# Delta-rule attention on one core: TensorE's projection work goes ahead of the second scores in slot 6, and ahead of the turned probabilities in slot 8

## The chip, the core and the metric

The program runs on one core of a Trainium2 chip. The metric is the device time of one execution in microseconds (us). The names of the engines in the profile: PE is TensorE (PEld its weight loads), DVE is VectorE, ACT is ScalarE, POOL is GpSimd, SP is SyncE.

## What is computed

Four layers with a residual each, on 1024 tokens of width 256: attention with a memory, a mixture of 16 experts, retention, and a mixture of 8 experts. Only the first is touched. Cut to what matters, with 16 heads of width 128 and segments of 64 tokens:

```python
def step(carry, seg):                       # 8 segments one after the other, 2 batches
    mem, z = carry
    qq, kk, vv = seg
    sigma_q = jax.nn.elu(qq) + 1.0
    scores = jnp.einsum('bhsk,bhtk->bhst', qq, kk) / scale
    scores = jnp.where(causal_mask, scores, -jnp.inf)
    att_dot = jax.nn.softmax(scores, axis=-1) @ vv
    att_mem = sigma_q @ mem / (sigma_q @ z)
    sigma_k = jax.nn.elu(kk) + 1.0
    delta = vv - sigma_k @ mem / (sigma_k @ z)
    mem_new = mem + jnp.einsum('bhsk,bhsv->bhkv', sigma_k, delta)
    z_new = z + sigma_k.sum(axis=-2, keepdims=True).transpose(0, 1, 3, 2)
    att = beta * att_mem + (1.0 - beta) * att_dot
    out = att.reshape(Bsz, SEG, H * DV) @ Wo
```

In front of it stand the projections of the normalised input to q, k and v.

## The kernel before

The attention goes through 8 stages, called 0 to 7 here: four turns, each with four heads, and two halves in each turn, one for each batch of 512 tokens. In the code `n = 2 * it + half` is the stage. The turns 1 and 2 are a loop in the program, turns 0 and 3 are written out.

A stage has 16 slots, `m` = 0 to 15, two for each of the 8 segments. The four heads are two groups `g` of two. Ahead of each slot TensorE reads the memory of one group (`read_memory`, L587) and adds the last segment's update to the memory of the other (`update_memory`, L597). This is the recurrence: ScalarE copies the memory out of its bank (L784), TensorE reads it, VectorE takes the reciprocal of the denominator (L911) and forms the difference from v (L917), TensorE updates.

A slot adds other work, which belongs to three stages at once:

- The stage itself: scores of two heads (`scores`, L608) in slots 0 and 6, into bank L[0]; VectorE masks them and takes the row's maximum in slots 1 and 7 (`mask_scores`, L927 and L932); GpSimd subtracts it (L469); ScalarE takes the exponential in slots 4 and 9 (L799); VectorE sums it in slots 5 and 10 (L936); GpSimd multiplies by the inverse (L478). TensorE turns these probabilities in slots 8 and 12 (`turn_probs`, L614), into L[0] and L[1], and ScalarE copies them in slots 9 and 13 (L804). TensorE multiplies them by v in slots 10 and 14 (L622).
- The stage behind: its readings are turned in slots 1 to 4 (L628), VectorE adds them one slot later (`add_reading`, L946), and its output projection is in slots 12 to 15 (L636).
- The stage ahead: `AHEAD_AT` gives projection unit u to slot u, for u = 0 to 11. A unit is six 128x512 matmuls (L233 to L235). Units 0 to 3 are the q of the four heads, 4 to 7 the k, 8 to 11 the four tiles of v. Slots 7 to 10 also turn the key feature of head 0 to 3 (`turn_sigma_k`, L574). Slot 7 is project 7, turn 0, and slot 8 is turn 1, project 8. Two banks serve all of this: units 0, 2, 4, 6 and 8 and turn 0 go to A[0], units 1, 3, 5 and 7 and turn 1 to A[1].

ScalarE empties the banks in the slot after (`copy_ahead`): of each q or k unit an exponential (L769) and a copy (L770), of a turned feature a copy (L778). VectorE forms the feature two slots after the unit (`sigma`, L889, then L902 for q, or L895 and L900 for k). The exponential of unit u goes to a buffer that unit u - 2 used, so ScalarE waits for the feature of unit u - 2.

Each engine takes its instructions in the order of the code. What TensorE waits for ahead of the steps that the change touches is:

```python
pe.wait_ge(qk_copied, 8 * n + u - 1)        # project, unit u = 2 to 7: the copy of unit u - 2
pe.wait_ge(skt_copied, 4 * n + 1)           # project, unit 8: the copy of turn 0
pe.wait_ge(qk_copied, 8 * n + h + 7)        # turn_sigma_k, h = 0, 1: the copy of unit 6, 7
pe.wait_ge(sigma_ready, 8 * n + h + 5)      # turn_sigma_k: VectorE's feature of that head
```

The second scores wait for `att_ready` (the fourth `add_reading`, VectorE's slot 5), and the turned probabilities for `masked` (L927 of VectorE's slot 7) and `p_ready`. Stage 0 has no stage behind, stage 7 none ahead.

Of the kernel before, what the change touches and what calls it, by code (L numbers as in the profile page):

```python
# [229 lines left out]
def split3(pe, out, stationary, moving, first, last, **kw):  # L230

    (sh, sl), (mh, ml) = stationary, moving
    pe.matmul(out, sh, mh, start=first, stop=False, **kw)  # L233
    pe.matmul(out, sh, ml, start=False, stop=False, **kw)  # L234
    return pe.matmul(out, sl, mh, start=False, stop=last, **kw)  # L235


def delta_attention(nc, outer, norm, carried, x, ident, ident_ready, scratch, x_in, Wq, Wk, Wv, Wo, betas, mask_in,
# [12 lines left out]
    with ExitStack() as ctx:  # L251
# [3 lines left out]
        def sem(name):  # L255
            signals.append(nc.alloc_semaphore(name=name))
            return signals[-1]

        def bank(name):
# [61 lines left out]
        sc_ready, masked, max_ready, shifted, exp_ready = (  # L321
            sem("scores_ready"), sem("scores_masked"), sem("max_ready"), sem("scores_shifted"), sem("exp_ready"))
        sum_ready, inv_ready, p_ready = sem("exp_sum_ready"), sem("exp_sum_inverted"), sem("probs_ready")
        pT_ready, pTs_ready, bt_ready, bt_copied = (
            sem("probsT_ready"), sem("probsT_copied"), sem("local_ready"), sem("local_copied"))
        at_ready, att_ready, wo_ready, y_copied = (
            sem("readingT_ready"), sem("attT_ready"), sem("out_ready"), sem("out_copied"))
# [38 lines left out]
        with nc.Block() as block:  # L366
# [154 lines left out]
            def _(pe):  # L521
# [13 lines left out]
                def project(n, half, u, free=None, at_start=None):  # L535

                    b = A[PROJECT_BANK[u]] if at_start is None else at_start
                    if free is not None:
                        pe.wait_ge(*free)
                    if u % 4 == 0:  # L540
                        pe.wait_ge(low_done, 3 * n + u // 4 + 1)
                    if at_start is not None:
                        pass
                    elif 2 <= u < 8:
                        pe.wait_ge(qk_copied, 8 * n + u - 1)
                    elif u == 8:
                        pe.wait_ge(skt_copied, 4 * n + 1)
                    elif u > 8:
                        pe.wait_ge(v_copied, 4 * n + u - 8)
                    for k in range(KD):  # L550
                        if u < 8:
                            i, h = u // 4, u % 4
                            cols = slice(half * HALF, (half + 1) * HALF)
                            last = split3(pe, b[:, :],
                                          (w_high[i][:, k, h * DK:(h + 1) * DK], w_low[i][:, k, h * DK:(h + 1) * DK]),
                                          (xh[:, k, cols], xl[:, k, cols]), k == 0, k == KD - 1)
                        else:
                            j = half * TPH + u - 8
                            last = split3(pe, b[:, :], (xh[:, k, j * P:(j + 1) * P], xl[:, k, j * P:(j + 1) * P]),
                                          (w_high[0][:, k, :], w_low[0][:, k, :]), k == 0, k == KD - 1)  # L560
                    last.then_inc(proj_ready, 1)
# [39 lines left out]
                def scores(n, half, pp):  # L601

                    for s in range(STEPS):
                        for hh in range(GROUP):
                            h, pair, par = GROUP * pp + hh, s // 2, s % 2
                            seg = slice((half * STEPS + s) * SEG, (half * STEPS + s + 1) * SEG)
                            at = (hh * TPH + pair) * SEG
                            last = pe.matmul(L[0][par * SEG:(par + 1) * SEG, at:at + SEG], qT[:, h, seg], kT[:, h, seg],  # L608
                                             start=True, stop=True)
                    last.then_inc(sc_ready, 1)  # L610

                def turn_probs(n, pp, hh):
                    for t in range(TPH):
                        last = pe.transpose(L[hh][:, t * P:(t + 1) * P], probs[:, hh * TPH + t, :], ident[:, :])  # L614
                    last.then_inc(pT_ready, 1)

                def local(n, half, pp, hh):

                    h = GROUP * pp + hh
                    pe.wait_ge(pTs_ready, 4 * n + h + 1)  # L620
                    for t in range(TPH):
                        last = pe.matmul(L[hh][:, t * P:(t + 1) * P], v[:, half * TPH + t, h * DK:(h + 1) * DK],  # L622
                                         pTs[hh][:, t * P:(t + 1) * P], start=True, stop=True)
                    last.then_inc(bt_ready, 1)

                def turn_reading(half, h):
                    for t in range(TPH):
                        last = pe.transpose(L[READINGS_BANK[h]][:, t * P:(t + 1) * P], read[:, half, h, t, :], ident[:, :])  # L628
                    last.then_inc(at_ready, 1)
# [10 lines left out]
                def slot(it, half, m, first, last):  # L640

                    n = 2 * it + half
                    ahead, behind = not (last and half), not (first and not half)
                    if m == 0:
                        if behind:
                            pe.wait_ge(bt_copied, 4 * n - 1)
                        scores(n, half, 0)
                    if m == 6:
                        if behind:
                            pe.wait_ge(att_ready, 4 * n)  # L650
                        pe.wait_ge(masked, 2 * n + 1)
                        scores(n, half, 1)
                    if behind and m in READINGS_AT:
                        h = READINGS_AT[m]
                        if h == 0:
                            pe.wait_ge(bt_copied, 4 * n)
                            for g in range(2):
                                pe.wait_ge(read_ready[g], STEPS * n)
                        elif h == 1:
                            pe.wait_ge(masked, 2 * n + 1)  # L660
                        else:
                            pe.wait_ge(att_ready, 4 * n - 4 + h - 1)
                        turn_reading(1 - half, h)
                    if m == 8:
                        pe.wait_ge(p_ready, 4 * n + 2)
                        pe.wait_ge(masked, 2 * n + 2)
                        turn_probs(n, 0, 0)
                        turn_probs(n, 0, 1)
                    if m == 12:
                        pe.wait_ge(p_ready, 4 * n + 4)  # L670
                        for hh in range(2):
                            pe.wait_ge(bt_copied, 4 * n + hh + 1)
                            turn_probs(n, 1, hh)
                    if m in (10, 14):
                        for hh in range(2):
                            local(n, half, (m - 10) // 4, hh)
                    if ahead:
                        for what, u in AHEAD_AT.get(m, ()):
                            if what == "turn":
                                turn_sigma_k(n + 1, 1 - half, u)  # L680
                                continue
                            free = None
                            if u == 0:
                                free = v_copied, 4 * n + 4
                            elif u == 1:

                                free = (skt_copied, 4 * n + 4) if first else (y_copied, n - 1)
                            project(n + 1, 1 - half, u, free)
                    out_at = OUT_AT if ahead else LAST_OUT_AT
                    if behind and m in out_at:  # L690
                        if m == min(out_at):
                            pe.wait_ge(att_ready, 4 * n)
                            if ahead:
                                pe.wait_ge(skt_copied, 4 * n + 8)
                            else:
                                pe.wait_ge(y_copied, n - 1)
                        project_out(1 - half, out_at[m])
# [36 lines left out]
                n = STAGES  # L734
# [1405 lines left out]
```

## Time and profile before

| | |
|---|---|
| time, median of 3 runs | 724.89 us (722.25 to 725.99) |
| span of the profiled execution, first to last instruction | 721.6 us |
| TensorE busy, matmuls | 659.8 us, 91% |
| VectorE busy | 405.8 us, 56% |
| ScalarE busy | 340.2 us, 47% |
| GpSimd busy | 309.3 us, 43% |
| a stage of the attention, stages 1 to 6 | 52.1 to 52.2 us |

Of the profiled execution the page gives the span alone, so this stands for its own time; it lies 3.3 us under the median and 0.65 us under the fastest of the three runs. The stage's length is the distance of the same instruction in neighbouring stages (L608 of slot 6 starts at 158.82, 211.01 and 263.12 us). Shares of the whole span are means over layers with different limits; the attention ends by about 450 us, and the change lies between 57 and 380 us.

### The profile page before, as it was taken

What the parts mean: (1) busy time and instruction counts of PE and PEld (TensorE: products, weight loads), DVE (VectorE), ACT (ScalarE), POOL (GpSimd) and SP (SyncE); (2) the same over time, 40 slices, a digit from 0 to 9 for tenths busy, and PEclk for the clock granted to TensorE, in tenths of its full rate; (3) what the DMA queues carried; (4) which work ended last, traced back from release to release, by engine and by line L of the source; (5) the groups of instructions that cost most, each with busy time, mean ns of one, the idle gap of its engine ahead of it and who ended that gap; (6) DMA issues with size and microseconds to landing.
All of it is one profiled execution on the core that took longest, in us unless ns stands there. A gap on an engine that the chain in (4) does not pass through costs nothing. (4 is left out here: it accounts for less than half of the span.)

```text
span 721.6 us, 12441 instructions
## 1 busy us (share of the span) xinstructions
PE 659.8 (91%) x4222; PEld 553.4 (77%) x4222; DVE 405.8 (56%) x1063; ACT 340.2 (47%) x836; POOL 309.3 (43%) x377
## 2 busy tenths in 40 slices
PE   3888999999999999999999997889999968996997
PEld 3767888988988979979979896776666556986754
DVE  6758487196295295494493646783222269555343
ACT  2655766567467567566566561323343321200221
POOL 4565462552453444353351111616666315200563
PEclk9999999999999999999999999799999979995999
DMA  8011010110210200200100131993233162009440
GB/s 263 30 41 49 30 32 30 55 36 7 64 32 2 65 29 0 65 29 12 55 1 1 42 78 65 334 368 95 92 94 90 52 216 80 1 29 365 135 121 23
DMA packets 29778, 57.90 MB, mean 80 GB/s; under 512 B 4670, under 2 KB 15904, under 8 KB 29728
## 3 DMA queue, kind: packets, MB, share of 16 engines
q1 hardware_dynamic: 22720, 42.03, 17.1%
q0 software_dynamic: 4896, 13.12, 6.2%
q10 hardware_dynamic: 2112, 2.10, 0.8%
q8 instruction: 30, 0.49, 0.3%
q14 instruction: 20, 0.16, 0.1%
HBM read 48.06 MB, written 10.09 MB: 81 GB/s over the span
## 5 line engine op out<-in xcount | busy, mean ns | idle before, releaser
L911 DVE RECIPROCAL denominators<-readings 128x2 f32<-128x2 f32 x128 | 21.2, 166 | 147.6 <-PE readings L587 146.9
L447 POOL TENSOR_TENSOR w_high<-xn,ones 128x256 fp32r<-128x256 f32 x84 | 53.9, 672 | 76.7 <-PE ahead L235 35.5
L587 PEld LDWEIGHTS readings<-memory_copy,sigma 128*128 128x128 f32 x512 | 75.2, 191 | 11.2 <-ACT memory_copy L784 2.2
L793 ACT ACTIVATE memory_reading<-readings,denominators 64x128 f32<-64x128 f32 x256 | 78.7, 357 | 6.0 <-DVE denominators L911 4.0
L587 PE MATMUL readings<-memory_copy,sigma 128*128 128x129 f32 x512 | 78.8, 276 | 2.2 <-ACT memory_copy L784 2.1
L784 ACT ACTIVATE memory_copy<-memory 128x258 f32<-128x258 f32 x128 | 50.2, 392 | 61.9 <-PE memory L597 47.9
L917 DVE SCALAR_TENSOR_TENSOR minus_delta<-readings,denominators,v 64x128 f32<-64x128 f32 x240 | 73.8, 347 | 4.5 <-DVE denominators L911 0.3
L597 PE MATMUL memory<-minus_delta,sigma_k_tokens 128*128 128x129 f32 x480 | 73.2, 275 | 0.0
L1221 POOL DMA_INDIRECT xs_e<-rows_e,gather_at_e x46 | 44.6, 969 | 54.3 <-DVE gather_at_e L1635 19.0
L1368 PE MATMUL up_e<-weights_e,xT_e 128*128 x184 | 66.4, 483 | 1.2 <-ACT xT_e L1497 1.2
L451 POOL TENSOR_TENSOR w_low<-xn,w_high 128x256 fp32r<-128x256 f32 x84 | 65.7, 813 | 1.6
L769 ACT ACTIVATE x<-ahead 128x512 f32<-128x512 f32 x60 | 35.9, 598 | 63.4 <-PE ahead L235 30.8
L636 PE MATMUL ahead<-wo,attT 128*128 128x256 f32 x256 | 64.4, 396 | 1.0 <-DVE attT L946 1.0
L597 PEld LDWEIGHTS memory<-minus_delta,sigma_k_tokens 128*128 128x128 f32 x480 | 63.0, 191 | 0.0
L1732 DVE TENSOR_TENSOR h_e<-gated_e,up_e 128x176 f32<-128x176 f32 x46 | 15.5, 338 | 80.7 <-ACT gated_e L1504 80.7
L478 POOL TENSOR_TENSOR xn<-scores,exp_sum_inverse 64x512 f32<-64x512 f32 x32 | 34.1, 1065 | 60.9 <-DVE exp_sum_inverse L938 59.1
L636 PEld LDWEIGHTS ahead<-wo,attT 128*128 128x128 f32 x256 | 58.9, 306 | 1.3 <-DVE attT L946 1.2
L1386 PE MATMUL down_e<-weights_e,hT_e 128*128 (+1 forms) x184 | 56.3, 405 | 0.0
L233 PE MATMUL ahead<-xh,w_high 128*128 128x512 f32 x120 | 53.0, 442 | 2.9 <-POOL w_low L451 1.9
L469 POOL TENSOR_TENSOR scores<-scores,score_max 128x512 f32<-128x512 f32 x16 | 16.8, 1048 | 82.4 <-DVE score_max L932 76.6
L1368 PEld LDWEIGHTS up_e<-weights_e,xT_e 128*128 128x128 f32 x184 | 31.2, 189 | 24.9 <-issue 15.0
L235 PE MATMUL ahead<-xh,w_low 128*128 128x512 f32 x120 | 48.0, 400 | 0.0
(282 smaller groups left out, 1444.6 us busy)
## 6 DMA issues: line engine op xcount, KB each, us to landing
weights_e<-experts SPq DMA_DIRECT2D x24, 608.0 KB, 12.1
xn<-L_attn_Wq SPq DMA_DIRECT2D x8, 512.0 KB, 3.9
xn<-L_attn_Wk SPq DMA_DIRECT2D x7, 512.0 KB, 3.8
xn<-L_attn_Wv SPq DMA_DIRECT2D x7, 512.0 KB, 3.8
wo<-L_attn_Wo SPq DMA_DIRECT2D x1, 2048.0 KB, 13.2
rows_e<-xn ACTq DMA_DIRECT2D x4, 512.0 KB, 10.4
x<-L_attn_x SPq DMA_DIRECT2D x4, 256.0 KB, 3.4
x<-L_attn_x SPq DMA_DIRECT2D x2, 512.0 KB, 3.5
```

The source lines that it names most:

```text
L233: pe.matmul(out, sh, mh, start=first, stop=False, **kw)
L235: return pe.matmul(out, sl, mh, start=False, stop=last, **kw)
L447: last = pool.tensor_tensor(w_high[i][:, :, of], w_stage[:, :, of], one, ALU.mult)
L451: last = pool.tensor_tensor(w_low[i][:, :, of], w_stage[:, :, of], fr(w_high[i][:, :, of]), ALU.subtract)
L587: last = pe.matmul(KQ[g][:, hh * MC:(hh + 1) * MC], sqk[:, GROUP * g + hh, pair, 2 * par:2 * par + 2, :], mz[g][:, hh, :], start=True, sto ...
L597: last = pe.matmul(MM[g][:, hh * MC:(hh + 1) * MC], skt[:, GROUP * g + hh, pair, :], dl[g][par][:, hh, :], start=False, stop=True, skip_gr ...
L636: last = pe.matmul(A[1][:, 0:D], rows[:, i::H], wo[:, i, :], start=(i == 0), stop=(i == H - 1))
L784: act.activation(mz[g][:, :, :], MM[g][:, 0:GROUP * MC].rearrange("p (h c) -> p h c", h=GROUP), ACT.Copy).then_inc(mem_copied[g], 1)
L793: last = act.activation(read[rows, half, GROUP * g + hh, pair, :], KQ[g][rows, hh * MC:hh * MC + DK], ACT.Copy, scale=nr[g][rows, hh:hh + 1])
L917: last = dve.scalar_tensor_tensor(out=dl[g][par][rows, hh, 0:DK], in0=KQ[g][rows, hh * MC:hh * MC + DK], scalar=nr[g][rows, hh:hh + 1], in ...
L1368: last = pe.matmul(GU[b % 2][:, 0:2 * INTER], xT[b % 2][:, k, :], flat[:, bass.ds(first + k * 2 * INTER, 2 * INTER)], start=k == 0, stop=k ...
L1386: last = pe.matmul(Y[b % 2][:, 0:D], hT[b % 2][0:count, k, :], flat[0:count, bass.ds(first + 4 * INTER + k * D, D)], start=k == 0, stop=k ...
```

## The change

In a slot with both, TensorE's second scores (slot 6) and first turns of probabilities (slot 8) now come behind the work for the stage ahead. Waits and instructions are the same, and no other engine's order differs.

```diff
--- before.py
+++ after.py
@@ -645,11 +645,6 @@
                         if behind:
                             pe.wait_ge(bt_copied, 4 * n - 1)
                         scores(n, half, 0)
-                    if m == 6:
-                        if behind:
-                            pe.wait_ge(att_ready, 4 * n)
-                        pe.wait_ge(masked, 2 * n + 1)
-                        scores(n, half, 1)
                     if behind and m in READINGS_AT:
                         h = READINGS_AT[m]
                         if h == 0:
@@ -661,11 +656,6 @@
                         else:
                             pe.wait_ge(att_ready, 4 * n - 4 + h - 1)
                         turn_reading(1 - half, h)
-                    if m == 8:
-                        pe.wait_ge(p_ready, 4 * n + 2)
-                        pe.wait_ge(masked, 2 * n + 2)
-                        turn_probs(n, 0, 0)
-                        turn_probs(n, 0, 1)
                     if m == 12:
                         pe.wait_ge(p_ready, 4 * n + 4)
                         for hh in range(2):
@@ -686,6 +676,16 @@
 
                                 free = (skt_copied, 4 * n + 4) if first else (y_copied, n - 1)
                             project(n + 1, 1 - half, u, free)
+                    if m == 6:
+                        if behind:
+                            pe.wait_ge(att_ready, 4 * n)
+                        pe.wait_ge(masked, 2 * n + 1)
+                        scores(n, half, 1)
+                    if m == 8:
+                        pe.wait_ge(p_ready, 4 * n + 2)
+                        pe.wait_ge(masked, 2 * n + 2)
+                        turn_probs(n, 0, 0)
+                        turn_probs(n, 0, 1)
                     out_at = OUT_AT if ahead else LAST_OUT_AT
                     if behind and m in out_at:
                         if m == min(out_at):
```

TensorE in slot 6 of a stage in the loop, before (readings and memory are the recurrence; ahead is the projection's bank, local the scores' bank; in brackets the semaphores that an instruction waits for):

```order
L597 MATMUL memory1<-minus_delta10,sigma_k_tokens 128x129 [waits delta_ready1]
L597 MATMUL memory1<-minus_delta10,sigma_k_tokens 128x129
L608 MATMUL local0<-kT,carried 64x64 [waits scores_masked,attT_ready]
L608 MATMUL local0<-kT,carried 64x64 x15
L545 REGISTER_ALU
L233 MATMUL ahead0<-xh,w_high1 128x512 [waits qk_copied]
```

The same place, of the change:

```order
L545 REGISTER_ALU
L233 MATMUL ahead0<-xh,w_high1 128x512 [waits qk_copied]
L234 MATMUL ahead0<-xl,w_high1 128x512
L235 MATMUL ahead0<-xh,w_low1 128x512
L233 MATMUL ahead0<-xh,w_high1 128x512
L234 MATMUL ahead0<-xl,w_high1 128x512
L235 MATMUL ahead0<-xh,w_low1 128x512
L608 MATMUL local0<-kT,carried 64x64 [waits scores_masked,attT_ready]
L608 MATMUL local0<-kT,carried 64x64 x15
L587 MATMUL readings1<-memory_copy1,sigma 128x129 [waits memory_copied1]
```

The 32 small matmuls of the scores, with their wait, now stand behind the six matmuls of unit 6 and directly ahead of slot 7's reading.

TensorE in slot 8 of that stage, before (xn holds the probabilities, sigma_k1 the key feature of head 1):

```order
L665 REGISTER_ALU
L666 REGISTER_ALU [waits probs_ready]
L614 MATMUL local0<-ident,xn 128x128 [waits scores_masked]
L614 MATMUL local0<-ident,xn 128x128 x3
L614 MATMUL local1<-ident,xn 128x128 x4
L569 REGISTER_ALU
L574 MATMUL ahead1<-ident,sigma_k1 128x128 [waits sigma_ready,qk_copied]
L574 MATMUL ahead1<-ident,sigma_k1 128x128 x3
L541 REGISTER_ALU
L547 ISA [waits w_split_done]
L233 MATMUL ahead0<-w_high0,xh 128x512 [waits sigma_k_copied]
```

The same place, of the change, from the last matmul of unit 8 on:

```order
L235 MATMUL ahead0<-w_high0,xl 128x512
L685 REGISTER_ALU
L686 REGISTER_ALU [waits probs_ready]
L614 MATMUL local0<-ident,xn 128x128 [waits scores_masked]
L614 MATMUL local0<-ident,xn 128x128 x3
L614 MATMUL local1<-ident,xn 128x128 x4
L587 MATMUL readings1<-memory_copy1,sigma 128x129 [waits memory_copied1]
```

Turn 1, with its wait for `qk_copied` (the copy of unit 7), and unit 8, with its wait for `sigma_k_copied` (the copy of turn 0), now stand directly behind slot 8's update, and the eight turns of the probabilities behind them.

## Rows read from the trace of the kernel before

**Rows 1.** The page's first lines: span, and TensorE's busy time

```profile
span 721.6 us, 12441 instructions
...
PE 659.8 (91%) x4222; PEld 553.4 (77%) x4222; DVE 405.8 (56%) x1063; ACT 340.2 (47%) x836; POOL 309.3 (43%) x377
```

**Rows 2.** Busy time by stretch: PE, PEld, DVE, ACT, POOL; then clock, DMA, GB/s

```profile
199.35:217.79 18.44, 17.50 (x136) 15.16 (x134) 17.66 (x42) 11.82 (x31) 9.49 (x11) 1.00 0.09 29
221.32:245.46 24.14, 24.14 (x159) 22.89 (x157) 7.34 (x26) 14.78 (x36) 12.22 (x18) 1.00 0.08 23
```

**Rows 3.** Timeline, TensorE, stage 3, slots 5 to 9: start, duration

```profile
209.80 0.61 PE L597 MATMUL memory<-minus_delta,sigma_k_tokens 128*128 128x129 f32 x4
211.01 1.20 PE L608 MATMUL local<-kT,carried 128*64 128x64 f32 x32 [0.60 <-DVE attT L946]
...
216.42 0.66 PE L574 MATMUL ahead<-ident,sigma_k 128*128 128x128 f32 x4 [0.34 <-ACT kT L770]
216.91 0.61 PE L587 MATMUL readings<-memory_copy,sigma 128*128 128x129 f32 x4
217.36 0.61 PE L597 MATMUL memory<-minus_delta,sigma_k_tokens 128*128 128x129 f32 x4
218.54 1.09 PE L614 MATMUL local<-ident,xn 128*128 128x128 f32 x8 [0.57 <-DVE scores L927]
...
221.32 0.61 PE L587 MATMUL readings<-memory_copy,sigma 128*128 128x129 f32 x4
```

**Rows 4.** Timeline, VectorE, stage 3, slots 6 and 7

```profile
214.82 0.43 DVE L900 COPY sigma<-sigma_k 128x512 f32<-128x512 f32 x1
...
217.34 0.43 DVE L900 COPY sigma<-sigma_k 128x512 f32<-128x512 f32 x1
217.79 0.69 DVE L927 SCALAR_TENSOR_TENSOR scores<-local,mask 128x512 f32<-128x512 f32 x1
```

**Rows 5.** Timeline, ScalarE, stage 3, slots 5 to 8

```profile
207.84 0.59 ACT L770 ACTIVATE kT<-ahead 128x512 f32<-128x512 f32 x1
...
215.28 0.60 ACT L769 ACTIVATE x<-ahead 128x512 f32<-128x512 f32 x1 [2.77 <-DVE sigma L900]
215.78 0.59 ACT L770 ACTIVATE kT<-ahead 128x512 f32<-128x512 f32 x1
...
217.80 0.60 ACT L769 ACTIVATE x<-ahead 128x512 f32<-128x512 f32 x1 [0.67 <-DVE sigma L900]
218.29 0.59 ACT L770 ACTIVATE kT<-ahead 128x512 f32<-128x512 f32 x1
218.77 0.60 ACT L778 ACTIVATE sigma_k_tokens<-ahead 128x512 f32<-128x512 f32 x1
```

**Rows 6.** Timeline, TensorE: slot 8's turns of the probabilities, stages 1 and 6

```profile
114.28 1.07 PE L614 MATMUL local<-ident,xn 128*128 128x128 f32 x8 [0.60 <-DVE scores L927]
...
374.92 1.06 PE L614 MATMUL local<-ident,xn 128*128 128x128 f32 x8 [0.60 <-DVE scores L927]
```

**Rows 7.** Timeline, stage 0, slots 7 to 9: TensorE, VectorE, ScalarE

```profile
65.94 1.63 PE L614 MATMUL local<-ident,xn 128*128 128x128 f32 x8 [2.58 <-DVE scores L927]
...
70.31 0.61 PE L587 MATMUL readings<-memory_copy,sigma 128*128 128x129 f32 x4
...
63.02 1.15 DVE L900 COPY sigma<-sigma_k 128x512 f32<-128x512 f32 x1
...
64.76 0.59 ACT L770 ACTIVATE kT<-ahead 128x512 f32<-128x512 f32 x1
65.24 0.60 ACT L778 ACTIVATE sigma_k_tokens<-ahead 128x512 f32<-128x512 f32 x1
```

**Rows 8.** Busy time by stretch, as rows 2: stage 0 and stage 3

```profile
64.00:66.00 2.00, 0.06 (x1) 0.09 (x2) 1.03 (x3) 1.73 (x4) 1.07 (x1) 1.00 0.71 241
66.00:68.00 2.00, 2.00 (x11) 2.00 (x12) 1.95 (x7) 0.74 (x3) 1.04 (x1) 0.57 0.00 0
...
216.00:218.00 2.00, 1.63 (x13) 1.36 (x12) 1.87 (x5) 1.33 (x5) 0.00 (x0) 1.00 0.00 0
```

## The prediction

> **What bounds the kernel now.** First the page: the span is 721.6 us and TensorE is busy 91% of it [rows 1]. TensorE looks like the bound, but that is a mean over four layers, and the change touches seven stages of one. So I read the timeline of one of them. Stage 3 stands for stages 1 to 6: slot 8's turned probabilities begin at 114.28 in stage 1 and at 374.92 in stage 6 [rows 6], which is 260.64 over five stages, 52.1 each.
>
> Busy time by stretch splits such a stage in two [rows 2]. From slot 9 to the next stage's slot 2 (221.32 to 245.46) TensorE is busy 24.14 of 24.14 us and VectorE 7.34: TensorE is the bound. From slot 2's end to slot 7 (199.35 to 217.79) VectorE is busy 17.66 of 18.44 and TensorE 17.50, with gaps: VectorE has become the bound. In this second part a wait of TensorE says only that TensorE is early for something of VectorE's; to start it on other work first ends nothing sooner unless VectorE, too, gets on.
>
> The timelines of the three engines show what TensorE meets there:
>
> - Slot 6: the update starts at 209.80 and the scores at 211.01, after 0.60 idle, for VectorE's L946 [rows 3]. A group of four such matmuls (two instructions) with work behind it takes 0.45 from start to start (216.91 to 217.36 [rows 3]), so without the wait they would have begun at 210.25: 0.76 is lost.
> - Slot 7: turn 0 waits 0.34 and starts at 216.42 [rows 3]. It needs the copy of unit 6, L770 from 215.78 for 0.59, until 216.37 [rows 5]. That stands behind unit 6's exponential, which started at 215.28 after 2.77 idle, for VectorE's L900 [rows 5] from 214.82 for 0.43, until 215.25 [rows 4].
> - Slot 8: the update starts at 217.36, the turned probabilities at 218.54 instead of 217.81 [rows 3]: 0.73 is lost. They waited for VectorE's mask, L927 from 217.79 for 0.69, until 218.48 [rows 4]. Slot 9 starts at 221.32 [rows 3].
>
> **The change, part by part.** No instruction is added or removed; six matmuls and 32 small ones change places in slot 6, eight turns change places with four turns and six matmuls in slot 8. No DMA and no other engine's queue is in it.
>
> *Slot 6.* Unit 6 needs the copy of unit 4, which was through at 207.84 + 0.59 = 208.43 [rows 5]; it starts at 210.25 with no wait. By the time that it is through, L946 has ended (it let the scores go at 211.01 [rows 3]), and the scores follow with none either. TensorE reaches the end of the slot 0.76 earlier. The scores themselves come a few tenths later, but VectorE takes them up only at 217.79 [rows 4], so that costs nothing; if VectorE were not so late, it would cost those tenths. Where do the 0.76 us go? To turn 0. Its chain (L900 until 215.25, exponential and copy on ScalarE until 216.37 [rows 4, 5]) has TensorE's unit 6 far behind it and is set by VectorE alone. VectorE was busy nearly without a break from slot 3 on [rows 2], and had no wait for TensorE to lose. So turn 0 stays at 216.42, and its wait grows from 0.34 to 1.10. Slot 6 is worth 0.00; at most 0.34 or 0.76 if VectorE's work itself shrank, for which I see no reason.
>
> *Slot 8.* The update still starts at 217.36, and from 217.81 TensorE is free. First in its queue is now turn 1. It needs the copy of unit 7: L770 from 218.29 for 0.59, until 218.88 [rows 5]. That again is VectorE's time: the exponential before it started at 217.80 after 0.67 idle, for L900, which ended at 217.34 + 0.43 = 217.77 [rows 4, 5]. With the 0.05 that lay between copy and turn in slot 7 (216.37 to 216.42), turn 1 starts at 218.93. Before, the first work started at 218.54, so the wait is 0.39 longer: the mask came out at 218.48, 0.40 before the copy. Queued behind turn 1 are unit 8, the turned probabilities, which could have run, and the recurrence's reading of slot 9, for which VectorE waits.
>
> Unit 8 needs the copy of turn 0: L778 from 218.77 for 0.60, until 219.37 [rows 5], so 219.42 at TensorE. Turn 1 takes 0.49 after a wait (turn 0: 216.42 to 216.91 [rows 3]), which is 218.93 to 219.42. This wait is just covered; without the turn ahead of it, it would cost another 0.49.
>
> The three pieces took 218.54 to 221.32 = 2.78 in the old order, the probabilities after a wait [rows 3]. In the new order it is turn 1 that follows a wait. I have no row for these pieces in the new order, so I bound them: 2.78 if the loss at a start just moves, 2.91 if turn 1's is added and the probabilities' is kept. With 2.85 slot 9 starts at 218.93 + 2.85 = 221.78 instead of 221.32: +0.46 a stage, between +0.39 and +0.52.
>
> Is it given back? From slot 9 on TensorE has no gap for 24 us [rows 2], so what it starts late, it ends late. The probabilities' copy in slot 9 stands behind the exponential of the scores, and the next wait of VectorE is for TensorE. The late start of VectorE's full stretch follows TensorE's reading in slot 2. All moves together: 6 stages x 0.46 = **+2.8** (2.3 to 3.1).
>
> *Stage 0* is another case. There the mask was late and the probabilities started at 65.94. Unit 7's copy ended at 64.76 + 0.59 = 65.35 and turn 0's at 65.24 + 0.60 = 65.84 [rows 7], behind L900 of VectorE that ended at 63.02 + 1.15 = 64.17 [rows 7]. So turn 1 starts at 65.40 and unit 8 at 65.89: 0.54 earlier, less 0.07 for the longer work, **-0.5**. Stage 7 has no stage ahead: 0.
>
> Sum: +2.8 - 0.5 = **+2.3**, so the profiled 721.6 would be 723.9. The profiled execution lies 3.3 below the median of the runs, and I take the sum as a difference: 724.9 + 2.3 = 727.2 us.
>
> The queue's order decides slot 8, and the row shows it: at 209.80 to 211.01 unit 6 was ready behind the waiting scores and did not pass them [rows 3, 5].
>
> The Trainium skill says so too (TensorE: Matmul & The Clock Gate, "Step-by-step: what each phase is for"): weight loads can be pulled forward, matmuls stay in program order. This speaks against the change, since the ready probabilities can't pass turn 1; were it otherwise, both orders would cost the same.
>
> **The rivals.**
>
> *The clock falls in slots 7 and 8.* In stage 0 TensorE was busy 0.06 of the two us to 66.00, and in the next two us its granted clock was 0.57 on the mean, of the levels 1.2 and 2.4 GHz [rows 8]. The same three pieces then took 65.94 to 70.31 = 4.37 [rows 7] instead of 2.78: a fall costs 1.59. In stage 3 the gap of slot 7 left 1.63 of two us busy, and the clock stayed at 1.00 [rows 8]. After the change they are 1.10 and 1.12, with 1.39 us of work between them (216.42 to 217.81), so under half of 3.6 us is busy. This lies between a row that kept the clock and one that lost it, and nothing in the attention lies nearer. One fall in six stages gives 728.8, two 730.4, all six 736.8. I would expect none to two.
>
> The Trainium skill (same page, "HAM oscillation — how this bites in real kernels") has idle time between bursts put TensorE back to the half rate again and again; by that rule the change is worse than my sum, by 1.59 for each fall.
>
> *The waits vanish and nothing takes their place: faster.* If the copies of units 6 and 7 came early enough (by 1.1 us each), stages 1 to 6 would give back 0.76 + 0.73 = 1.49 each, 8.9 in all, and stage 0 half a microsecond more: 715.5. For it speaks that both waits are real and the ready work is real. Against it, both copies wait for VectorE's L900 in their rows [rows 5], and VectorE is full [rows 2]. It decides from the point where unit 7's copy ends before the mask, 0.40 earlier than now; at that point stage for stage is 0.
>
> *No change.* VectorE could have slack from slot 9 that takes up 0.46 a stage, or the copies come a bit earlier in the new rhythm. Then only stage 0 remains: 724.4.
>
> **How the numbers follow.** Slot 8 late, clock kept: 0.43, 727.2 us, its own range 726 to 729. Slot 8 late and one or more falls of the clock: 0.36, 728.8 to 732. No change: 0.13. Faster: 0.05, 715.5 to 721. The rest, 0.03, is more falls. The measurement tells about 0.5%, 3.6 us, from no change, so 721.3 to 728.5 is "same". The first case lies in it for the most part, the second beyond it: slower 0.40, same 0.53, faster 0.07 (the runs of before are themselves 3.7 apart). The range reaches from 723.5, below no change, to 731.5, two falls and the upper bound of slot 8.
>
> **What would show it.** Right: no idle time ahead of L608 in slot 6 and of L614 in slot 8; ahead of L574 in slot 7 about 1.1 us, put down to L770; ahead of L574 in slot 8 about 1.1 us, put down to L770; from the update of slot 8 to slot 9's reading 4.4 instead of 3.96 (217.36 to 221.32); a stage of 52.6 instead of 52.1. Wrong: L900 of slots 6 and 7 earlier relative to slot 3's reading, or a stage that is not longer. The clock: rows of 0.5 behind slot 8 in stages 1 to 6, and L233 of unit 8 with 0.6 to 0.8 us for one instead of 0.4 to 0.5.

## The result and the profile after

The changed kernel takes 727.62 us (median of 20 runs, 723.46 to 731.05), the kernel before 724.11 (20 runs, 720.33 to 726.60). The ratio is 1.0041, with a 95% interval of 1.0022 to 1.0060: 3.0 us slower, between 1.6 and 4.3. The forecast was 727.2. The ratio compares runs taken side by side and is not the quotient of the two medians, which differ by 3.5 us. The span of the profiled execution is 725.6 us, against 721.6 [rows 1]; the time of that execution is 727.4. So a time is not its span: in the executions of this case that have both, it is 1.7 to 2.9 us above it, 1.8 in most. The 3.3 us between the profiled span before and the median are therefore mostly this, and the execution itself lay about 1.5 us below the median (an estimate: 721.6 + 1.8 = 723.4). The forecast was a difference, so it does not suffer from it.

First TensorE's timeline of stage 3, the rows that answer to [rows 3] (start, duration, what ended the idle time before):

```profile
211.27 0.61 PE L597 MATMUL memory<-minus_delta,sigma_k_tokens 128*128 128x129 f32 x4
211.63 0.47 PE L233 MATMUL ahead<-xh,w_high 128*128 128x512 f32 x1
...
213.20 1.20 PE L608 MATMUL local<-kT,carried 128*64 128x64 f32 x32
...
217.88 0.65 PE L574 MATMUL ahead<-ident,sigma_k 128*128 128x128 f32 x4 [1.00 <-ACT kT L770]
218.37 0.61 PE L587 MATMUL readings<-memory_copy,sigma 128*128 128x129 f32 x4
218.82 0.61 PE L597 MATMUL memory<-minus_delta,sigma_k_tokens 128*128 128x129 f32 x4
220.39 0.66 PE L574 MATMUL ahead<-ident,sigma_k 128*128 128x128 f32 x4 [0.96 <-ACT kT L770]
220.88 0.50 PE L233 MATMUL ahead<-w_high,xh 128*128 128x512 f32 x1
...
222.37 1.04 PE L614 MATMUL local<-ident,xn 128*128 128x128 f32 x8
223.24 0.61 PE L587 MATMUL readings<-memory_copy,sigma 128*128 128x129 f32 x4
```

- Slot 6: unit 6 (211.63) follows the update (211.27) by 0.36, and the scores (213.20) wait for nothing. The wait of 0.60 is gone. The scores start 1.93 behind the update instead of 1.21, and VectorE still takes them up only at 219.25 (L927, below).
- Slot 7: turn 0 now waits 1.00 instead of 0.34, for the same L770. From the update of slot 6 to turn 0 it is 217.88 - 211.27 = 6.61, before 216.42 - 209.80 = 6.62 [rows 3]. All that slot 6 saved is in that wait.
- Slot 8: from the update (218.82) TensorE waits until turn 1 at 220.39, for L770 once more. Unit 8 and the turned probabilities (222.37) follow without a gap. Update to slot 9's reading: 223.24 - 218.82 = 4.42, before 3.96 [rows 3].

The engines that it waits for, in the same stage (VectorE, then ScalarE):

```profile
218.79 0.43 DVE L900 COPY sigma<-sigma_k 128x512 f32<-128x512 f32 x1
219.25 0.69 DVE L927 SCALAR_TENSOR_TENSOR scores<-local,mask 128x512 f32<-128x512 f32 x1
```

```profile
217.23 0.59 ACT L770 ACTIVATE kT<-ahead 128x512 f32<-128x512 f32 x1
...
219.75 0.59 ACT L770 ACTIVATE kT<-ahead 128x512 f32<-128x512 f32 x1
220.22 0.61 ACT L778 ACTIVATE sigma_k_tokens<-ahead 128x512 f32<-128x512 f32 x1
```

They answer to [rows 4] and [rows 5]. The feature of unit 5 ends at 218.79 + 0.43 = 219.22, the mask at 219.94, the copy of unit 7 only at 219.75 + 0.59 = 220.34, and turn 1 starts 0.05 behind it. The mask was ready 0.45 before turn 1 started. The copy of turn 0 ends at 220.22 + 0.61 = 220.83, and unit 8 starts at 220.88.

Busy time by stretch (columns as in [rows 2]: PE, PEld, DVE, ACT, POOL, then clock, DMA share and GB/s), stage 0 and stage 3:

```profile
64.00:66.00 2.00, 0.00 (x0) 0.00 (x0) 1.93 (x3) 1.00 (x3) 0.63 (x1) 1.00 0.49 179
66.00:68.00 2.00, 1.86 (x7) 1.51 (x8) 1.93 (x8) 1.95 (x6) 1.04 (x1) 0.70 0.00 0
...
217.00:219.00 2.00, 1.12 (x10) 1.12 (x11) 1.90 (x5) 1.58 (x5) 0.00 (x0) 1.00 0.00 0
219.00:221.00 2.00, 1.04 (x9) 0.77 (x9) 1.90 (x5) 1.75 (x4) 0.26 (x1) 1.00 0.00 0
```

In stage 3 TensorE is busy 1.12 and 1.04 of two us, where it was 1.63 in slot 7 [rows 8], and the clock stays at 1.00. In stage 0 it falls, as before.

How the loss adds up is best seen by the same reading in all stages. Slot 12's reading, in stages 0 and 6, before and then after:

```profile
79.85 0.61 PE L587 MATMUL readings<-memory_copy,sigma 128*128 128x129 f32 x4
...
387.22 0.61 PE L587 MATMUL readings<-memory_copy,sigma 128*128 128x129 f32 x4
```

```profile
80.23 0.61 PE L587 MATMUL readings<-memory_copy,sigma 128*128 128x129 f32 x4
...
390.73 0.61 PE L587 MATMUL readings<-memory_copy,sigma 128*128 128x129 f32 x4
```

A stage grew from 307.37 / 6 = 51.23 to 310.50 / 6 = 51.75 us, by 0.52; in six stages 3.1. (These six distances hold slots 12 to 15 of stage 0, all of 1 to 5, and slots 0 to 11 of stage 6.)

### The profile page after: what moved, and what is told of

Read it like the earlier page. It is cut to its first block and busy times, and to the rows that moved or that the text cites. A ratio compares the mean times of both kernels' runs of the same rounds, so it can differ in the third digit from the quotient of the medians.

```text
span 725.6 us, 12441 instructions
## 1 busy us (share of the span) xinstructions
PE 659.4 (91%) x4222; PEld 550.5 (76%) x4222; DVE 405.6 (56%) x1063; ACT 339.7 (47%) x836; POOL 309.6 (43%) x377
```

## The experiments

The table has, for each kernel, the ratio to the kernel before with its 95% interval (against the runs of it taken beside that kernel, whose medians were 724.11, 724.19, 723.67 and 723.80), the start of slot 12's reading in stages 0 and 6 of the profiled execution, and a sixth of their distance, the length of a stage.

| kernel | median us | ratio (interval) | slot 12, stage 0 and 6 | a stage |
|---|---|---|---|---|
| before | 724.11 | 1 | 79.85, 387.22 | 51.23 |
| changed | 727.62 | 1.0041 (1.0022 to 1.0060) | 80.23, 390.73 | 51.75 |
| changed, again | 727.06 | 1.0056 (1.0027 to 1.0085) | 77.39, 387.74 | 51.73 |
| slot 6 alone | 724.31 | 1.0003 (0.9980 to 1.0027) | 78.22, 385.49 | 51.21 |
| slot 8 alone | 727.38 | 1.0059 (1.0038 to 1.0080) | 80.46, 390.81 | 51.73 |
| unit 8 first | 729.92 | 1.0105 (1.0070 to 1.0139) | 78.14, 391.29 | 52.19 |
| before, with space | 724.19 | 1.0009 (0.9986 to 1.0033) | 77.42, 384.80 | 51.23 |
| changed, with space | 720.51 | 0.9955 (0.9932 to 0.9977) | 75.59, 381.60 | 51.00 |
| the same, unit 8 first | 720.89 | 0.9959 (0.9940 to 0.9979) | 77.45, 383.44 | 51.00 |
| the same, units 8 and 9 first | 716.92 | 0.9902 (0.9867 to 0.9938) | 74.51, 376.43 | 50.32 |
| the last, slot 6 as before | 719.38 | 0.9929 (0.9901 to 0.9957) | 75.64, 378.94 | 50.55 |

The length of a stage tells the kernels apart to some hundredths of a microsecond, since it leaves out the start of the program, the first twelve slots of stage 0 and the layers behind; the ratio holds them all. Each kernel has one trace, the changed one two.

### One edit at a time

Slot 6 alone: the block of slot 8 goes back to its old place.

```diff
                     if behind and m in READINGS_AT:
...
+                    if m == 8:
+                        pe.wait_ge(p_ready, 4 * n + 2)
+                        pe.wait_ge(masked, 2 * n + 2)
+                        turn_probs(n, 0, 0)
+                        turn_probs(n, 0, 1)
                     if m == 12:
```

> Only slot 6 is changed (unit 6 ahead of the second scores), slot 8 is as before. Theory (both orders of slot 6 end at the copy of unit 6, which VectorE's feature of unit 4 releases): slot 7's reading comes 0.8 us earlier, turn 0's wait grows from 0.34 to 1.1 us, slot 8's reading is where it was; 0.0 a stage, ratio 1.000 +- 0.002. Rival one (slot 6 carries part of the loss, since the scores come later or the clock falls in the longer gap): slower by 1 to 3 us. Rival two (the wait ahead of the scores is really saved, and slot 8 alone loses more than it): faster by 0.76 x 6 = 4.6 us.

Measured: 1.0003, a stage of 51.21 us, the clock at 1.00 in stages 1 to 6. TensorE's timeline of stage 3:

```profile
208.12 0.61 PE L597 MATMUL memory<-minus_delta,sigma_k_tokens 128*128 128x129 f32 x4
...
210.04 1.20 PE L608 MATMUL local<-kT,carried 128*64 128x64 f32 x32
...
214.74 0.66 PE L574 MATMUL ahead<-ident,sigma_k 128*128 128x128 f32 x4 [1.01 <-ACT kT L770]
...
215.68 0.61 PE L597 MATMUL memory<-minus_delta,sigma_k_tokens 128*128 128x129 f32 x4
216.85 1.09 PE L614 MATMUL local<-ident,xn 128*128 128x128 f32 x8 [0.57 <-DVE scores L927]
```

The scores have no wait, turn 0 waits 1.01 for the copy of unit 6, and 6.62 us after the update (214.74 - 208.12) all is as in the kernel before. Slot 8 waits its old 0.57 for the mask. Slot 6's edit is worth nothing, and both rivals fall.

Slot 8 alone: the block of slot 6 goes back instead.

```diff
+                    if m == 6:
+                        if behind:
+                            pe.wait_ge(att_ready, 4 * n)
+                        pe.wait_ge(masked, 2 * n + 1)
+                        scores(n, half, 1)
                     if behind and m in READINGS_AT:
```

> Only slot 8 is changed (turn 1 and unit 8 ahead of the turned probabilities), slot 6 is as before. Theory: the whole loss of the change is here. Turn 1 starts 0.05 us behind the copy of unit 7, slot 8's update to slot 9's reading is 4.4 us instead of 3.96, +0.5 a stage in stages 1 to 6, +3 us in all, ratio 1.004. Rival (the loss needs both edits, since only together they leave two gaps of 1 us close to each other): less than half of it, ratio 1.000 to 1.002.

Measured: 1.0059, a stage of 51.73, +0.50. Its timeline shows the old wait in slots 6 and 7 and the new one in slot 8:

```profile
212.63 1.20 PE L608 MATMUL local<-kT,carried 128*64 128x64 f32 x32 [0.60 <-DVE attT L946]
...
218.04 0.66 PE L574 MATMUL ahead<-ident,sigma_k 128*128 128x128 f32 x4 [0.34 <-ACT kT L770]
...
218.98 0.61 PE L597 MATMUL memory<-minus_delta,sigma_k_tokens 128*128 128x129 f32 x4
220.55 0.66 PE L574 MATMUL ahead<-ident,sigma_k 128*128 128x128 f32 x4 [0.96 <-ACT kT L770]
...
223.41 0.61 PE L587 MATMUL readings<-memory_copy,sigma 128*128 128x129 f32 x4
```

Turn 0 waits 0.34, turn 1 0.96, and from the update at 218.98 to slot 9's reading it is 4.43. So the whole loss is here, with no help from slot 6.

### What heads the queue in slot 8

```diff
-        AHEAD_AT |= {7: [("project", 7), ("turn", 0)], 8: [("turn", 1), ("project", 8)],
+        AHEAD_AT |= {7: [("project", 7), ("turn", 0)], 8: [("project", 8), ("turn", 1)],
```

> The changed kernel with unit 8 ahead of turn 1 in slot 8: unit 8, turn 1, turned probabilities. Theory (slot 8 starts with the release of what heads TensorE's queue): unit 8 waits for the copy of turn 0, which ends 0.49 us behind the copy of unit 7, and nothing covers that now. Slot 8's update to slot 9's reading: 4.8 us; against the changed kernel +0.36 to +0.49 a stage, 6 stages, so +5 to +6 us against the kernel before, ratio 1.007 to 1.008. Rival (what counts is that the projection goes first, not which copy it waits for): as the changed kernel, ratio 1.004.

Measured: 1.0105, a stage of 52.19, 0.96 more than before and 0.44 to 0.46 more than with the change. Six stages make 5.8 us, as expected; the ratio lies above the expected 1.007 to 1.008, but its interval (1.0070 to 1.0139, six runs) reaches down to it.

```profile
217.57 0.61 PE L597 MATMUL memory<-minus_delta,sigma_k_tokens 128*128 128x129 f32 x4
219.64 0.50 PE L233 MATMUL ahead<-w_high,xh 128*128 128x512 f32 x1 [1.46 <-ACT sigma_k_tokens L778]
...
222.44 0.61 PE L587 MATMUL readings<-memory_copy,sigma 128*128 128x129 f32 x4
```

Unit 8 waits for L778, the copy of turn 0, which leaves the update 4.87 us from slot 9's reading. The 0.49 us by which this copy is later than that of unit 7 is now paid almost in full, where the change covered it with turn 1. Same work, three orders, and each starts with the release of its first item.

### Making the copies early

In the kernel before, the exponential of unit u overwrites that of unit u - 2, so those of units 6 and 7 wait for VectorE's features of units 4 and 5. The copied probabilities' space `pTs` is idle from slot 14 to slot 9. Two of the eight exponentials go there, and the buffers of units 6 and 7 have been free since the features of units 2 and 3. The copy of the first probabilities in slot 9 now has to wait until VectorE has made the feature of unit 5, which reads that space:

```diff
+        exp_at = e + e + pTs + e
...
-                        if u >= 2:
-                            act.wait_ge(sigma_ready, 8 * n + u - 1)
-                        act.activation(e[u % 2][:, :], bank[:, :], ACT.Exp)
+                        if u >= 2 and u not in (4, 5):
+                            act.wait_ge(sigma_ready, 8 * n + u - (1 if u < 4 else 3))
+                        act.activation(exp_at[u][:, :], bank[:, :], ACT.Exp)
...
-                def copy_probs(n, pp):
+                def copy_probs(n, pp, ahead):
+                    if ahead and not pp:
+                        act.wait_ge(sigma_ready, 8 * n + 14)
```

In VectorE's `sigma`, `e[u % 2]` becomes `exp_at[u]`. First in the kernel before:

> The kernel before, with the exponentials of units 4 and 5 written to the space of the copied probabilities, which is free then. So ScalarE's exponentials of units 6 and 7 no longer wait for VectorE's features of units 4 and 5, but for those of units 2 and 3. Order of TensorE as before. Theory: turn 0's wait of 0.34 us in slot 7 goes, but slot 8's turned probabilities still wait for VectorE's mask, which has not moved: slot 9's reading 0.0 earlier, ratio 0.999 to 1.000. Rival (the copies are the bound in either order): 0.3 a stage, 2 us faster, ratio 0.997.

Measured: 1.0009, a stage of 51.23, the same to the hundredth. In slots 7 and 8:

```profile
213.50 0.60 PE L575 MATMUL ahead<-ident,sigma_k 128*128 128x128 f32 x4
...
216.12 1.10 PE L615 MATMUL local<-ident,xn 128*128 128x128 f32 x8 [1.13 <-DVE scores L930]
...
218.88 0.61 PE L588 MATMUL readings<-memory_copy,sigma 128*128 128x129 f32 x4
```

Turn 0 has no wait any more, and the turned probabilities wait 1.13 for VectorE's mask instead of 0.57. The time moved from one wait to the next, as in slot 6. (L614 and L574 are L615 and L575 here.) The rival falls.

Then in the changed kernel:

> The changed kernel, with the exponentials of units 4 and 5 in the space of the copied probabilities, so that those of units 6 and 7 don't wait for VectorE's features of units 4 and 5. Theory (the copies of units 6 and 7 are what the change puts at the head of the queue): turn 0 starts with the feature of unit 4 (1.1 us earlier), turn 1 with the feature of unit 5, 1.1 us earlier than in the changed kernel, and slot 9's reading about 0.65 us earlier than in the kernel before, 1.1 earlier than in the changed one: 6 stages, ratio to the kernel before 0.994 to 0.996. Rival (VectorE's own order is the whole bound and ScalarE's copies only follow it): no more than the changed kernel, ratio 1.004.

Measured: 0.9955, a stage of 51.00.

```profile
210.62 0.63 PE L575 MATMUL ahead<-ident,sigma_k 128*128 128x128 f32 x4
...
213.14 0.63 PE L575 MATMUL ahead<-ident,sigma_k 128*128 128x128 f32 x4 [0.99 <-DVE sigma L903]
...
215.87 0.61 PE L588 MATMUL readings<-memory_copy,sigma 128*128 128x129 f32 x4
...
217.18 0.63 PE L575 MATMUL ahead<-ident,sigma_k 128*128 128x128 f32 x4 [0.25 <-DVE sigma L903]
...
219.03 0.61 PE L588 MATMUL readings<-memory_copy,sigma 128*128 128x129 f32 x4
```

Turn 0 has no wait, and turn 1 is released by VectorE's feature itself. To see what came of it I compare the shift of the readings against the kernel before. Slot 6's and slot 10's there, then slot 6's here:

```profile
209.35 0.61 PE L587 MATMUL readings<-memory_copy,sigma 128*128 128x129 f32 x4
...
224.04 0.61 PE L587 MATMUL readings<-memory_copy,sigma 128*128 128x129 f32 x4
```

```profile
204.58 0.61 PE L588 MATMUL readings<-memory_copy,sigma 128*128 128x129 f32 x4
```

In slot 6 the shift is 4.77 us (209.35 and 204.58), in slot 9 5.45 (221.32 and 215.87), so 0.68 was gained, as expected. In slot 10 it is 5.01 (224.04 and 219.03): 0.44 has gone back in slot 9, where turn 2 waits for VectorE's feature of unit 6. So 0.23 a stage is left, 1.4 us in six, where I had expected the gain of slot 8 to last. That the ratio of 0.9955, 3.3 us, fell into the expected range is luck. What the profiled execution gains beside this is in stage 0, 1.9 us: slot 8's reading to slot 10's took 8.77 us (59.97 to 68.74) instead of 10.71 (62.31 to 73.02). There the clock did not fall:

```profile
64.00:66.00 2.00, 1.70 (x16) 1.51 (x13) 1.93 (x8) 1.64 (x5) 1.04 (x1) 1.00 0.00 0
```

Before it was 0.57 [rows 8]. With slot 6 alone, whose copies are as late as before, the clock stayed at 1.00 too, and the same stretch took 8.39 us (62.98 to 71.37). So most of this term is the clock of stage 0. The early copies may have a part in it, since TensorE's wait ahead of slot 8's first matmul is 0.85 us there and 2.28 with the change; no run separates the two. The last section has the waits of all kernels.

Units first in slot 8, and then in slots 8 and 9:

```diff
-        AHEAD_AT |= {7: [("project", 7), ("turn", 0)], 8: [("turn", 1), ("project", 8)],
-                     9: [("turn", 2), ("project", 9)], 10: [("turn", 3), ("project", 10)], 11: [("project", 11)]}
+        AHEAD_AT |= {7: [("project", 7), ("turn", 0)], 8: [("project", 8), ("turn", 1)],
+                     9: [("project", 9), ("turn", 2)], 10: [("turn", 3), ("project", 10)], 11: [("project", 11)]}
```

> The changed kernel with the space of the copied probabilities for two exponentials, and unit 8 ahead of turn 1 in slot 8, but slot 9 as it was (turn 2 ahead of unit 9). Theory (what heads TensorE's queue in slot 9 gives the gain of slot 8 back): slot 9's reading comes earlier still, 0.9 us against the kernel before, but turn 2 behind it waits for VectorE's feature of unit 6, and slot 10's reading is where it was without the exchange, 0.2 us a stage earlier than before; ratio 0.995 to 0.996. Rival (the gain of 0.9 a stage comes from slot 8 alone): ratio 0.990.

> The same with units 8 and 9 ahead of turns 1 and 2 in slots 8 and 9. With the earlier copies unit 8 needs nothing that VectorE has yet to do in slot 7, so it runs while VectorE makes the feature of unit 5 and the mask. Theory: the 1.1 us wait ahead of slot 8's turn 1 is filled with unit 8; slot 9's reading 1.5 us earlier than in the kernel before, of which VectorE's slot 9 and the copies of the probabilities take some back: 1.0 a stage, 6 us, ratio 0.990 to 0.993. Rival (VectorE, full until 221.8 us in stage 3, takes it all back in slots 9 and 10): ratio 0.995 as without the exchange.

Measured: with slot 8 alone 0.9959 and 51.00, nothing more; with both slots 0.9902 and 50.32, 0.91 a stage under the kernel before. TensorE's timeline with slot 8 alone, and then with both:

```profile
214.68 0.50 PE L233 MATMUL ahead<-w_high,xh 128*128 128x512 f32 x1 [0.67 <-ACT sigma_k_tokens L779]
...
219.04 0.63 PE L575 MATMUL ahead<-ident,sigma_k 128*128 128x128 f32 x4 [0.49 <-DVE sigma L903]
```

```profile
210.42 0.50 PE L233 MATMUL ahead<-w_high,xh 128*128 128x512 f32 x1 [0.68 <-ACT sigma_k_tokens L779]
...
213.22 0.61 PE L588 MATMUL readings<-memory_copy,sigma 128*128 128x129 f32 x4
...
215.51 0.60 PE L575 MATMUL ahead<-ident,sigma_k 128*128 128x128 f32 x4
```

With slot 8 alone, slot 9's reading comes 0.94 us earlier than before, counted from slot 6's, as expected, but turn 2's wait for VectorE grows to 0.49: VectorE has taken the gain back one slot later. With unit 9 ahead of turn 2 as well, it has none, and the only wait left in slots 6 to 9 is unit 8's 0.68 for the copy of turn 0. The rival (VectorE takes it all back) falls. The way there was not the expected one, though: slot 9's reading is 0.94 earlier (213.22 - 202.19 = 11.03 behind slot 6's, before 221.32 - 209.35 = 11.97), not 1.5, and nearly all of it lasts. Six stages give 5.5 of the 7 us of the ratio; in the profiled execution the clock stayed at 1.00 in stage 0, too. At 716.92 us this kernel beats both of the case.

At last slot 6 back in its old order, with all the rest:

> Space for two exponentials, units 8 and 9 ahead of turns 1 and 2, but in slot 6 the second scores ahead of unit 6, as before. Theory (slot 6 was worth nothing only because turn 0 waited for a late copy of unit 6): with the early copies the 0.76 us lost ahead of the scores are on the path; slot 9's reading comes about 0.6 us later than with both edits, ratio 0.994 to 0.996. Rival (slot 6's order is worth nothing in any case, since VectorE gives back what it saves): as with both edits, ratio 0.990.

Measured: 0.9929 (0.9901 to 0.9957), between the rival's 0.990 and the expected 0.994 to 0.996; a stage of 50.55, 0.23 longer than with both edits.

```profile
205.39 1.20 PE L609 MATMUL local<-kT,carried 128*64 128x64 f32 x32 [0.59 <-DVE attT L949]
...
212.17 0.50 PE L233 MATMUL ahead<-w_high,xh 128*128 128x512 f32 x1 [0.41 <-ACT sigma_k_tokens L779]
```

The scores wait 0.59 again, and unit 8's wait shrinks from 0.68 to 0.41, so a part of slot 6's order is still hidden. With the copies early it is worth 0.23 a stage, where the change had 0.00 to 0.02 of it; I expected 0.6. The stages tell it; the intervals of the two ratios overlap.

### The changed kernel again

> The changed kernel once more, for a trace of another execution: the same ratio, 1.004 (1.002 to 1.006). Theory: turn 1 of slot 8 again starts 0.05 us behind the copy of unit 7, and the clock stays at 1.00 in stages 1 to 6. Rival (the clock falls in slots 7 and 8 in part of the executions): in this trace or in the other ones with this slot 8, one or more stages show unit 8's matmuls at 0.63 us instead of 0.40.

Measured: 1.0056, a stage of 51.73. Turn 1 again stands behind the copy. In the traces of the changed kernel (two), of slot 8 alone and of unit 8 first, no stage from 1 to 6 had a granted clock under 1.00 (busy time by stretch, 80 to 400 us: 1.00 in all four). The rival of the falling clock has nothing for it in 24 such stages.

## Why the prediction was right

- **Slot 6 is worth 0.00**: right. Turn 0's wait was forecast at 1.10 and is 1.00, and slot 6 alone shows 51.21 against 51.23.
- **Slot 8 costs 0.46, between 0.39 and 0.52**: right in the place, the cause and, in stage 3, the size: turn 1 starts 1.57 behind the update instead of 1.18, the 0.39 of the forecast, and the three pieces take 2.85 (220.39 to 223.24), the middle of its bounds. Over the stages slot 8's reading to slot 9's grew by 0.46 (stages 3 and 4) to 0.56 (stage 6), 2.98 in all six; I don't know why stages 1 and 6 pay more. The stage grew by 0.52, 0.50 and 0.50 in three traces, so six stages gave 3.0 to 3.1 instead of 2.8.
- **Nothing is given back from slot 9 on**: right; slot 12's readings carry the sum to the end.
- **Stage 0 gains 0.5**: right in sign, too large. Slot 8's reading to slot 9's was 8.00 us (62.31 to 70.31) and is 7.84, 7.75 and 7.64 in the three traces with the edit, so 0.16 to 0.36 was gained. This is the term that was mis-sized, and its smaller values are hardly clear of the spread: with TensorE's old order and only the space for two exponentials the stretch took 7.90. Turn 1's start lay 3.33 us behind slot 8's reading (66.14 - 62.81) instead of the 3.09 worked out, and the work behind it took 4.51 instead of 4.37 + 0.07 = 4.44, with the clock low in both. The first part is in VectorE's rows: the feature of unit 5 ended 2.10 us behind slot 8's reading instead of 1.86, since its L895 took 1.42 us there and 1.10 before. GpSimd is at work beside it in both, so what made it longer stays open.
- **The sum** was +2.3; with 3.1 and -0.16 it is +2.9, and the ratio says +3.0.
- **The matmuls keep their order**: right. In slot 8 the probabilities were ready (mask at 219.94) and stood behind turn 1 until 222.37.
- **The clock falls in slots 7 and 8**: did not happen in any stage traced. It had 0.36 of the chance, too much. Behind idle time the clock did fall in stage 0 (0.70 in the two us behind a wait of 2.28); behind the waits of 1.00 and 0.96 in stage 3 it stayed at 1.00. The section of the Trainium skill that the forecast names for this (TensorE: Matmul & The Clock Gate, "HAM oscillation — how this bites in real kernels") tells of DMA waits several times as long as these two, so it gave less reason for a fall here than I took from it.
- **Faster, if the copies came early**: that mechanism is real. With them early the same order gives a stage of 51.00, against 51.75 with late copies and 51.23 in the old order with either, so the chain that I held against this rival, through the exponential's buffer, is what turned the gain into a loss. But its price was wrong: I gave 1.49 a stage, and 0.23 came, since VectorE's features stand behind the copies, in slot 9 too.

TensorE's first timeline with 0.76 and 0.73 us lost in slots 6 and 8 looks as if there were 1.5 us a stage to win. Both waits end with VectorE's work, in a stretch where VectorE is busy 96% [rows 2], and as long as the copies hang on VectorE too, other work put ahead only changes which of its results TensorE waits for. The order was worth something (0.91 a stage) only when the copies were early and units 8 and 9 stood first.

## What to carry over

Before moving ready work ahead of a waiting instruction, write down when each input of the moved work is ready as well. Here that was 0.40 us later than what the old order waited for, and in an in-order queue the later one costs its difference. A wait that another engine ends is not filled by work that waits for the same engine; look for what ties that work to it (here a buffer with two places), free that, and only then change the order.

## What the runs showed beside this

The granted clock behind slot 8's wait in stage 0 is not the same in all traces. With slot 6 alone, stage 0's slot 8 is the order of the kernel before. Its rows:

```profile
65.90 1.06 PE L614 MATMUL local<-ident,xn 128*128 128x128 f32 x8 [1.86 <-DVE scores L927]
...
68.65 0.61 PE L587 MATMUL readings<-memory_copy,sigma 128*128 128x129 f32 x4
```

```profile
64.00:66.00 2.00, 0.14 (x2) 0.13 (x2) 1.94 (x3) 0.88 (x2) 0.75 (x1) 1.00 0.55 194
66.00:68.00 2.00, 2.00 (x16) 1.85 (x17) 1.93 (x8) 1.95 (x6) 1.05 (x1) 1.00 0.00 0
```

TensorE is busy 0.14 of two us, then goes on at 1.00: the three pieces take 2.75 us (65.90 to 68.65). In the kernel before, it was 0.06, then 0.57, and 4.37 us [rows 7, 8]. The work is the same; 1.62 us lie between them. The wait is not the same: it is 1.86 us here and was 2.58 there, and in the two us ahead (62 to 64) TensorE was busy 2.00 here and 1.37 there. Over the eleven traces it sorts the same way. The clock fell behind waits of 2.76, 2.58, 2.50, 2.28, 2.19 and 2.09 us (unit 8 first, before, before with space, changed, changed again, slot 8 alone), and stayed behind 1.86 (slot 6 alone) and in the four kernels that have early copies and the changed slot 8, whose longest wait in stage 0's slots 8 and 9 was 1.18. No run sets this wait on purpose, and whether slot 6 alone would keep the clock in every execution is open.

The start of the program varies more: the first reading of the memory, ahead of which neither the change nor the experiments touch the order, starts at 38.60 us before, 38.77 after, 36.34 with the change again and 39.58 with slot 8 alone. I take these two to make up much of the 6 to 8 us between the fastest and the slowest of the 20 runs of each kernel; no run tried it. The length of a stage leaves both out, and so shows a difference that single times can't.
